# Weighting and adding both expert choices on VectorE after the expert blocks, with GpSimd left to gather

## The chip, the cores and the metric

The kernel runs on one core of one Trainium2 chip. The metric is the device time of one execution in microseconds (us), as the median of several runs. The profile comes from one execution of its own. Lines such as L723 are lines of the kernel before.

## What is computed

Two layers over x (1354 rows of 256 floats), each added to its input:

```python
x = x + attention(layernorm(x), adj, ...)          # softmax(q k^T / 16 + 2 adj) v
x = x + moe(layernorm(x))                          # 8 experts, each row goes to 2

scores = xf @ router_w + router_b
topk_p, topk_i = top_k(softmax(scores), 2)
h = xf @ w1[e] + b1[e]
y = (silu(h @ wg[e] + bg[e]) * (h @ wv[e] + bv[e])) @ w2[e] + b2[e]
out = sum over the two chosen experts of gate * y
```

The change is in the last line: the two gated expert results of each row are added to x.

## The kernel before

The rows are held in 11 tiles of up to 128 rows (`TILES`; the last tile has 74 rows). The attention part ends with each row's two experts known; a row's first choice is the one with the lower expert number, its second choice the one with the higher. Each row is scattered twice into `expert_rows`, sorted by expert, and the rows of an expert fill blocks of 128. `BLOCKS` is 29, the most that any routing can need; where a routing needs fewer, the steps that are left repeat the last block.

The expert part is a loop over the blocks, `experts(s)`, written out on each engine and kept in step by semaphores. TensorE (PE) multiplies block s by the expert's fused gate and up matrices (`bT` against `weights`), transposes the gated result of block s-1 and multiplies block s-2 by the down matrix (`gT` against `weights`, counted by `y_mm`). VectorE (DVE) adds the biases, forms the gated product and the low parts of the split operands, and at L1780 adds the last bias into `ysum` (counted by `y_sum`). ScalarE (ACT) does silu and the high parts, and issues at L982 the store of `ysum` to `expert_out` (`ys`, counted by `y_out`).

GpSimd (POOL) first splits the experts' weights (`product_lo`, `down_lo`). Then it gathers: for choice k = 0 and all tiles, and then for choice k = 1 and all tiles, it reads from `needs` how many blocks must have been stored, waits for `y_out`, and issues at L723 an indirect DMA that brings each row's result into `picked[:, t, k, :]` (semaphore `gathered[t][k]`). Between these gathers it runs `add_first(t)`, three tiles behind the gathers: `picked` times the gate in place (L707), and then that added to `x1` (L710). The semaphore `part_added` counts both steps.

VectorE runs its whole block loop first. Then come eleven calls of `add_second(t)`, one instruction each (L1743): x1 = picked * gate + x1 for the second choice, after `gathered[t][1]` and `part_added`. It counts `added`.

SyncE (SP) writes the result in three stores: tiles 0 to 4 when `added` is 5, tiles 5 to 9 when it is 10 (both L543, 640 KB each), and the last tile with its 74 rows when it is 11 (L546, 74 KB). It then waits for all three:

```python
HALF = TILES // 2
for t in (0, HALF):
    sp.wait_ge(added, t + HALF)
    sp.dma_start(out[...], x1[:, t:t + HALF, :]).then_inc(result_out, 16)
sp.wait_ge(added, TILES)
sp.dma_start(out[span(TILES - 1, LAST), :], x1[:LAST, TILES - 1, :]).then_inc(result_out, 16)
sp.wait_ge(result_out, 48)
```

Of the kernel before, what the change touches and what calls it, by code (L numbers as in the profile page):

```python
# [6 lines left out]
ALU = mybir.AluOpType  # L7
# [40 lines left out]
def attention_then_top2_experts(  # L48
# [4 lines left out]

    N, D = x.shape
    E, _, H = w1.shape
    TOPK = 2
    TILES = -(-N // P)
# [29 lines left out]
    def width(t):  # L87
        return LAST if t == TILES - 1 else P
# [4 lines left out]
    with ExitStack() as ctx:  # L93
        def sem(name):
            return ctx.enter_context(nc.semaphore(name))
# [23 lines left out]
        x1 = keep.place("x1", [P, TILES, D])  # L119
# [41 lines left out]
        gates = keep.place("gates", [P, TOPK, TILES])  # L161
# [100 lines left out]
        picked = moe.place("picked", [P, TILES, TOPK, D])  # L262
# [70 lines left out]
        gathered = [[sem(f"gathered{t}_{k}") for k in range(TOPK)] for t in range(TILES)]  # L333
        part_added, added, result_out = sem("part_added"), sem("added"), sem("result_out")
# [26 lines left out]
        def finish_factors(wait_ge, engine, g, queue):  # L361

            mean, _, var, y, tmp, shift = factors_of(g)
            count = 14 * g

            def step(ins):
                nonlocal count
                count += 1
                ins.then_inc(newton1, 1)
                wait_ge(newton1, count)  # L370
            wait_ge(rough1, 2 * g + 2)
            for _ in range(3):
                step(engine.tensor_tensor(tmp, y, y, ALU.mult))
                step(engine.tensor_tensor(tmp, tmp, var, ALU.mult))
                step(engine.tensor_scalar(tmp, tmp, -0.5, 1.5, ALU.mult, ALU.add))
                step(engine.tensor_tensor(y, tmp, y, ALU.mult))
            step(engine.tensor_tensor(tmp, mean, y, ALU.mult))
            step(engine.tensor_scalar(shift, tmp, -1.0, None, ALU.mult))
            queue.sem_inc(factors_done)
# [171 lines left out]
        def _(pool):  # L551
            G = nc.gpsimd
# [147 lines left out]
                product_lo(e)  # L700
                down_lo(e)

            def add_first(t):

                n = width(t)
                pool.wait_ge(gathered[t][0], 16)
                G.tensor_scalar(picked[:n, t, 0, :], picked[:n, t, 0, :], gates[:n, 0, t:t + 1], None, ALU.mult  # L707
                                ).then_inc(part_added, 1)
                pool.wait_ge(part_added, 2 * t + 1)
                G.tensor_tensor(x1[:n, t, :], x1[:n, t, :], picked[:n, t, 0, :], ALU.add).then_inc(part_added, 1)  # L710


            for k in range(TOPK):
                for t in range(TILES):
                    if k == 0 and t >= 3:
                        add_first(t - 3)
                    if k == 1 and t < 3:
                        add_first(TILES - 3 + t)
                    n = width(t)
                    done = pool.value_load(needs[0:1, k, t:t + 1], min_val=1, max_val=BLOCKS)  # L720
                    pool.wait_ge(y_out, 16 * done)
                    pool.sem_inc(pool_passed)
                    pool.indirect_dma_start(  # L723
                        out=picked[:n, t, k, :], out_offset=None, in_=ys,
                        in_offset=bass.IndirectOffsetOnAxis(ap=ypos_i[:n, t, k:k + 1], axis=0)
                    ).then_inc(gathered[t][k], 16)
# [628 lines left out]
        def _(dve):  # L1355
            V = nc.vector
# [27 lines left out]
            def rough_factors(g):  # L1384
                _, var, half, y, _, _ = factors_of(g)
                V.tensor_scalar(half, var, EPS, None, ALU.add).then_inc(rough1, 1)
                dve.wait_ge(rough1, 2 * g + 1)
                rough_rsqrt(y, half).then_inc(rough1, 1)
# [347 lines left out]
            gate_weights()  # L1736
            dve.sem_inc(tables_done)

            def add_second(t):
                n = width(t)  # L1740
                dve.wait_ge(gathered[t][1], 16)
                dve.wait_ge(part_added, 2 * t + 2)
                V.scalar_tensor_tensor(x1[:n, t, :], picked[:n, t, 1, :], gates[:n, 1, t:t + 1],  # L1743
                                       x1[:n, t, :], ALU.mult, ALU.add).then_inc(added, 1)

            def bias_part(e, p):
                return tile_of(bias[:, :, B_AT[p]:B_AT[p] + B_SIZES[p]], e % B_SLOTS, P)
# [34 lines left out]
            for s in range(BLOCKS + 2):  # L1782
                experts(s)
            for t in range(TILES):
                add_second(t)


# [21 lines left out]
```

## Time and profile before

| | |
|---|---|
| time, median of 3 runs | 422.5 us (420.83 to 422.7) |
| the profiled execution's own time | 422.16 us |
| its span from first to last instruction | 420.4 us |
| TensorE busy | 383.6 us, 91% of the span |
| VectorE busy | 310.5 us, 74% |
| GpSimd busy | 277.3 us, 66% |
| ScalarE busy | 178.5 us, 42% |

The span is what the trace shows; the execution's own time is 1.7 us longer. The median is another 0.3 us above that execution. A busy share is an average over the whole span: it doesn't tell which engine sets the end of the last stretch, and the change lies in that stretch.

### The profile page before, as it was taken

The numbers are of one execution on the slowest core, as the hardware profiler recorded it, in microseconds if no ns is written. First come the engines' busy times: TensorE is split into PE (matmuls) and PEld (weight loads), VectorE is DVE, ScalarE is ACT, GpSimd is POOL, SyncE is SP. The second block draws the span as 40 slices with busy tenths as digits, with TensorE's granted clock in tenths as the row PEclk, the third lists the DMA queues.
The fourth block names the chain that finished last, engine by engine and source line by source line (L and its number), as shares of the span: only waits on it lengthen the run. The fifth ranks groups of instructions, "written<-read, shape, count | busy, mean of one in ns | idle before, by whom it ended". The sixth has DMA issues, their size and how long they took to land.

```text
span 420.4 us, 8132 instructions
## 1 busy us (share of the span) xinstructions
PE 383.6 (91%) x2273; PEld 331.5 (79%) x2273; DVE 310.5 (74%) x737; ACT 178.5 (42%) x312; POOL 277.3 (66%) x303
## 2 busy tenths in 40 slices
PE   1899989999999999999999696799899999999980
PEld 1788869879889889899788475688788888888870
DVE  4686887977779889698896994577576766676754
ACT  1375584463653553554453362453233223333310
POOL 3743949977386596596597650896986740577771
PEclk9899999999999999999999998899999999999996
DMA  6871569878879789688769956547764722233245
GB/s 209 304 276 51 170 222 326 268 202 269 263 222 301 242 245 322 219 258 268 216 215 339 372 171 209 209 140 245 276 248 150 274 87 74 88 92 90 69 128 177
DMA packets 54485, 89.43 MB, mean 213 GB/s; under 512 B 4658, under 2 KB 34810, under 8 KB 53420
## 3 DMA queue, kind: packets, MB, share of 16 engines
q1 hardware_dynamic: 43044, 75.33, 53.6%
q10 hardware_dynamic: 8776, 8.03, 5.9%
q0 software_dynamic: 2624, 5.56, 4.5%
q8 instruction: 21, 0.34, 0.3%
q14 instruction: 20, 0.16, 0.1%
HBM read 56.13 MB, written 32.77 MB: 211 GB/s over the span
## 4 chain that ended last, share of the span: by engine, by line
PE 64%; DVE 12%; DMA 9%; issue 7%; POOL 4%; POOLq 1%; ACT 1%; DVEq 1%; ACTq 0%
PE ps L997 25%; PE ps L1306 19%; PE ps L1201 6%; DMA xblk<-expert_rows 3%; DVE acc L1418 3%; PE ps L1203 3%; PE ps L1149 2%; PE ps L1340 2%; DMA expert_out<-ysum 2%; PE ps L1282 1%; DMA picked<-expert_out,ypos_i 1%; PE ps L1051 1%; DMA expert_rows<-xn_all,posi_all 1%; POOL picked L723 1%; POOLq L720 1%
## 5 line engine op out<-in xcount | busy, mean ns | idle before, releaser
L592 POOL TENSOR_TENSOR lo<-raw,hi 128x512 fp32r<-128x512 f32 x62 | 80.9, 1333 | 53.1 <-DVE acc L1418 48.7
L1306 PE MATMUL ps<-weights,bT_hi 128*128 x232 | 73.2, 397 | 0.0
L997 PE MATMUL ps<-hi,w1T_lo 128*128 128x512 f32 x128 | 53.1, 414 | 1.1 <-DVE w1T_lo L1359 1.0
L1306 PE MATMUL ps<-weights,bT_lo 128*128 x116 | 49.2, 425 | 2.1 <-DVE bT_lo L1359 2.1
L997 PE MATMUL ps<-hi,w1T_hi 128*128 128x512 f32 x128 | 50.7, 396 | 0.0
L1306 PEld LDWEIGHTS ps<-weights,bT_hi 128*128 128x128 f32 x232 | 44.5, 192 | 7.8
L997 PE MATMUL ps<-lo,w1T_hi 128*128 128x512 f32 x128 | 50.4, 394 | 0.0
L1201 PE MATMUL ps<-v,pT_hi 128*128 128x256 f32 (+3 forms) x242 | 44.8, 286 | 0.7 <-DVE pT_lo L1359 0.7
L1754 DVE TENSOR_TENSOR ps<-ps,bias 128x512 f32<-128x512 f32 x29 | 20.3, 699 | 32.6 <-PE ps L1306 25.2
L1418 DVE SCALAR_TENSOR_TENSOR acc<-raw,b1T,acc 128x512 f32<-128x512 f32 x48 | 42.0, 874 | 1.4
L1306 PE MATMUL ps<-weights,gT_hi 128*128 x232 | 42.7, 282 | 0.0
L723 POOL DMA_INDIRECT picked<-expert_out,ypos_i x22 | 22.7, 1031 | 28.2 <-DMA expert_out<-ysum 20.7
L731 ACT ACTIVATE bT_hi<-ps 128x256 fp32r<-128x256 f32 x29 | 11.2, 385 | 70.4 <-PE ps L1282 70.4
L1201 PEld LDWEIGHTS ps<-v,pT_hi 128*128 128x128 f32 (+3 forms) x242 | 36.9, 186 | 0.9 <-DVE pT_lo L1359 0.9
L731 ACT ACTIVATE ring<-ps 128x512 f32<-128x512 f32 x28 | 16.7, 595 | 48.0 <-PE ps L997 46.5
L1306 PE MATMUL ps<-weights,gT_lo 128*128 x116 | 35.2, 304 | 1.5 <-DVE ysum L1780 1.5
L1306 PEld LDWEIGHTS ps<-weights,gT_hi 128*128 128x128 f32 x232 | 36.0, 190 | 0.0
L681 POOL TENSOR_TENSOR weights<-landed,weights 128x2048 fp32r<-128x2048 f32 x7 | 32.2, 4605 | 3.3 <-ACT weights L731 2.9
L1203 PE MATMUL ps<-v,pT_lo 128*128 128x256 f32 (+3 forms) x121 | 34.1, 282 | 0.0
L617 POOL DMA_INDIRECT expert_rows<-xn_all,posi_all x22 | 24.9, 1132 | 8.9 <-issue 4.8
L731 ACT ACTIVATE hi<-raw 128x2048 fp32r<-128x2048 f32 x16 | 30.4, 1899 | 0.0
L1359 DVE TENSOR_TENSOR pT_lo<-ps,pT_hi 128x512 fp32r<-128x512 f32 (+5 forms) x44 | 20.3, 502 | 12.5 <-ACT pT_hi L731 12.5
(226 smaller groups left out, 969.2 us busy)
## 6 DMA issues: line engine op xcount, KB each, us to landing
expert_rows<-zeros SPq DMA_DIRECT2D x11, 1024.0 KB, 10.4
raw<-in_L_ffn_wg SPq DMA_DIRECT2D x8, 1024.0 KB, 6.5
raw<-in_L_ffn_wv SPq DMA_DIRECT2D x8, 1024.0 KB, 7.4
products<-ring SPq DMA_DIRECT2D x28, 256.0 KB, 5.6
landed<-products SPq DMA_DIRECT2D x7, 1024.0 KB, 7.6
adj_sb<-in_adj SPq DMA_DIRECT2D x10, 677.0 KB
bias<-biases SPq DMA_DIRECT2D x8, 640.0 KB, 5.2
w1raw<-in_L_ffn_w SPq DMA_DIRECT2D x8, 512.0 KB, 5.3
```

Source lines behind the costliest of these rows:

```text
L592: G.tensor_tensor(lo[j % RAWS][:, k, :], raw[j % RAWS][:, k, :], r32(hi[j % HIS][:, k, :]), ALU.subtract).then_inc(m_lo, 1)
L617: pool.indirect_dma_start(out=xs, out_offset=bass.IndirectOffsetOnAxis(ap=posi_all[:n, t, k:k + 1], axis=0), in_=xn2_all[:n, t, :], in_off ...
L681: G.tensor_tensor(weights[:, e % SLOTS, AT_LO:AT_LO + C_SIZE], landed[:, e % SLOTS, AT_LO:AT_LO + C_SIZE], r32(weights[:, e % SLOTS, AT_HI ...
L723: pool.indirect_dma_start(out=picked[:n, t, k, :], out_offset=None, in_=ys, in_offset=bass.IndirectOffsetOnAxis(ap=ypos_i[:n, t, k:k + 1], ...
L731: return nc.scalar.activation(o, i, ACT.Copy)
L997: last = nc.tensor.matmul(o, a, b, start=begins and n == 0, stop=ends and n == len(m) - 1)
L1201: nc.tensor.matmul(ps[:n, MIX, 0:D], pT[0][:w, k, :n], v[:w, k, i, :], start=k == 0 and i == 1, stop=False)
L1203: last = nc.tensor.matmul(ps[:n, MIX, 0:D], pT[1][:w, k, :n], v[:w, k, 0, :], start=False, stop=k == TILES - 1)
L1306: last = nc.tensor.matmul(o, stationary[i][:, k, :], part(e, ats[j] + k * width, width), start=n == 0, stop=n == len(m) - 1)
L1359: return V.tensor_tensor(o, a, b, ALU.subtract)
L1418: V.scalar_tensor_tensor(acc[j % ACCS][:, :], buf[:, k, :], b1T[:, e * KH + k:e * KH + k + 1], first_row[:, :] if k == 0 else acc[j % ACCS ...
L1754: V.tensor_tensor(ps[:, BANK_G[s % 2], :], ps[:, BANK_G[s % 2], :], bias_part(e_gu, 0), ALU.add).then_inc(g_sum, 1)
```

## The change

GpSimd keeps the 22 gathers and loses its 22 arithmetic instructions. VectorE's eleven `add_second` become 22 calls of `add_choice`: after the block loop it adds the first choice of all 11 tiles, and then the second choice of all 11. The instruction is the same for both. `part_added` now counts VectorE's first-choice adds, and only the second-choice adds wait for it. `added`, on which the stores wait, still counts the second-choice adds alone.

```diff
-            def add_first(t):
-                n = width(t)
-                pool.wait_ge(gathered[t][0], 16)
-                G.tensor_scalar(picked[:n, t, 0, :], picked[:n, t, 0, :], gates[:n, 0, t:t + 1], None, ALU.mult
-                                ).then_inc(part_added, 1)
-                pool.wait_ge(part_added, 2 * t + 1)
-                G.tensor_tensor(x1[:n, t, :], x1[:n, t, :], picked[:n, t, 0, :], ALU.add).then_inc(part_added, 1)
             for k in range(TOPK):
                 for t in range(TILES):
-                    if k == 0 and t >= 3:
-                        add_first(t - 3)
-                    if k == 1 and t < 3:
-                        add_first(TILES - 3 + t)
                     n = width(t)
                     done = pool.value_load(needs[0:1, k, t:t + 1], min_val=1, max_val=BLOCKS)
                     pool.wait_ge(y_out, 16 * done)
...
-            def add_second(t):
-                n = width(t)
-                dve.wait_ge(gathered[t][1], 16)
-                dve.wait_ge(part_added, 2 * t + 2)
-                V.scalar_tensor_tensor(x1[:n, t, :], picked[:n, t, 1, :], gates[:n, 1, t:t + 1],
-                                       x1[:n, t, :], ALU.mult, ALU.add).then_inc(added, 1)
+            def add_choice(t, k):
+                n = width(t)
+                dve.wait_ge(gathered[t][k], 16)
+                if k == 1:
+                    dve.wait_ge(part_added, t + 1)
+                V.scalar_tensor_tensor(x1[:n, t, :], picked[:n, t, k, :], gates[:n, k, t:t + 1],
+                                       x1[:n, t, :], ALU.mult, ALU.add).then_inc(added if k else part_added, 1)
...
             for s in range(BLOCKS + 2):
                 experts(s)
             for t in range(TILES):
-                add_second(t)
+                add_choice(t, 0)
+            for t in range(TILES):
+                add_choice(t, 1)
```

## Rows read from the trace of the kernel before

**Rows 1.** The page's head: the span, and each engine's busy time.

```profile
span 420.4 us, 8132 instructions
PE 383.6 (91%) x2273; PEld 331.5 (79%) x2273; DVE 310.5 (74%) x737; ACT 178.5 (42%) x312; POOL 277.3 (66%) x303
```

**Rows 2.** The chain that ended last, 398 to 421 us: start, length, what.

```profile
410.78 5.59 DMA picked<-expert_out,ypos_i
416.40 0.48 DVE x L1743
```

**Rows 3.** Timeline of GpSimd, 290 to 421 us: start, length, instruction, [idle before].

```profile
365.65 1.02 POOL L723 DMA_INDIRECT picked<-expert_out,ypos_i  x1 [0.61 <-issue]
366.72 0.93 POOL L707 TENSOR_SCALAR picked<-picked,gates 128x256 f32<-128x256 f32 x1
367.73 0.74 POOL L710 TENSOR_TENSOR x<-x,picked 128x256 f32<-128x256 f32 x1
369.08 1.02 POOL L723 DMA_INDIRECT picked<-expert_out,ypos_i  x1 [0.61 <-issue]
...
402.01 0.96 POOL L723 DMA_INDIRECT picked<-expert_out,ypos_i  x1 [0.31 <-issue]
403.27 0.95 POOL L723 DMA_INDIRECT picked<-expert_out,ypos_i  x1 [0.30 <-issue]
```

**Rows 4.** Timeline of VectorE after its block loop.

```profile
410.16 0.42 DVE L1780 TENSOR_TENSOR ysum<-ps,bias 128x256 f32<-128x256 f32 x1 [2.22 <-DMA expert_out<-ysum]
410.50 4.04 DVE L1743 SCALAR_TENSOR_TENSOR x<-picked,gates,x 128x256 f32<-128x256 f32 x10
416.40 0.48 DVE L1743 SCALAR_TENSOR_TENSOR x<-picked,gates,x 74x256 f32<-74x256 f32 x1 [1.86 <-DMA picked<-expert_out,ypos_i]
```

**Rows 5.** By tile `gates`: the add's duration, ns min/median/max.

```profile
L1743 DVE SCALAR_TENSOR_TENSOR x<-picked,gates,x x11: 474/476/483, 410.5 to 416.4; 128x256 f32<-128x256 f32 x10, 74x256 f32<-74x256 f32 x1
```

**Rows 6.** Windows: each engine's busy time in one stretch, clock, DMA share, GB/s.

```profile
352.00:399.90 47.90, 47.90 (x299) 41.88 (x298) 32.78 (x59) 15.83 (x30) 31.88 (x35) 1.00 0.29 87
```

**Rows 7.** Groups of VectorE by form, 352 to 363 us, then 364 to 399 us.

```profile
L1768 DVE TENSOR_TENSOR gated<-ps,silu 128x512 f32<-128x512 f32 x2 | 1.4, 691 | 0.1
...
L1768 DVE TENSOR_TENSOR gated<-ps,silu 128x512 f32<-128x512 f32 x7 | 4.8, 691 | 0.2
```

**Rows 8.** Timeline: last down multiply and `ysum`, of block 25 and of 29.

```profile
394.75 0.40 PE L1306 MATMUL ps<-weights,gT_hi 128*128 x2
...
395.37 0.42 DVE L1780 TENSOR_TENSOR ysum<-ps,bias 128x256 f32<-128x256 f32 x1
...
409.55 0.40 PE L1306 MATMUL ps<-weights,gT_hi 128*128 x2
```

**Rows 9.** By tile `out`: the result's stores, issue ns, first and last start.

```profile
L543 SPq DMA_DIRECT2D out<-x x2: 388/388/388, 412.6 to 414.6; - x2
L546 SPq DMA_DIRECT2D out<-x x1: 299/299/299, 416.9 to 416.9; - x1
```

**Rows 10.** Windows over the stores: the last two figures are DMA share and GB/s.

```profile
413.40:413.80 0.40, 0.00 (x0) 0.00 (x0) 0.40 (x2) 0.00 (x0) 0.00 (x0) 0.50 0.78 207
...
417.20:417.40 0.20, 0.00 (x0) 0.00 (x0) 0.00 (x0) 0.00 (x0) 0.00 (x0) 0.50 1.02 343
417.40:417.60 0.20, 0.00 (x0) 0.00 (x0) 0.00 (x0) 0.00 (x0) 0.00 (x0) 0.50 0.41 133
...
418.60:419.40 0.80, 0.00 (x0) 0.00 (x0) 0.00 (x0) 0.00 (x0) 0.00 (x0) 0.50 0.23 79
419.40:419.80 0.40, 0.00 (x0) 0.00 (x0) 0.00 (x0) 0.00 (x0) 0.00 (x0) 0.50 0.05 18
```

**Rows 11.** DMA issues: a 74-row gather (388 to 392 us), and all 22.

```profile
picked<-expert_out,ypos_i POOLq DMA_INDIRECT x1, 4.8
...
picked<-expert_out,ypos_i POOLq DMA_INDIRECT x22, 2.9
```

**Rows 12.** Waits of VectorE, 399 to 421 us: in total, times, longest.

```profile
DVE ysum L1780 <- DMA expert_out<-ysum: 3.0, 2, 2.2
```

## The prediction

> **What bounds the kernel now.** The page's head comes first [rows 1]: TensorE is busy 91% of the span, VectorE 74%, GpSimd 66%. That is an average, and the change touches the end alone, so the question is who sets the end. The chain that ended last gives it [rows 2]: its last two pieces are the landing of the last gather (issued 410.78, landed 416.37) and one VectorE add behind it. The reader is to see that this gather is the only add's input that came late. The timeline of GpSimd says why it was issued so late [rows 3]: in the first choice's part a gather comes every 3.43 us (365.65 against the next at 369.08, which the three rows between fill: 1.02 gather, 0.93 multiply, 0.74 add, and the gaps), in the second choice's part every 1.25 us (402.01, 403.27). GpSimd is never caught up from 365 us on.
>
> VectorE is in its block loop until 410.58, then does ten adds at one go, waits 1.86 us for the gather, does the eleventh and ends at 416.88 [rows 4]. The windows say what the block loop is bound by [rows 6]: from 352.0 to 399.9 TensorE is busy 47.90 of 47.90 us at the full granted clock. And the stores say what comes last [rows 9, 10]: two of 640 KB issued at 412.6 and 414.6, one of 74 KB at 416.9, and the span ends at 420.43, 3.5 us after that last issue.
>
> **What the change removes.** 11 multiplies and 11 adds leave GpSimd, 11 x (0.94 + 0.74) = 18.5 us of its time [rows 3]. No block waits for them. The gathers come no later than now, since each has less in front of it. The worst case is the present one: issued 410.78, landed 416.37, and the add that needs it now stands 22nd in VectorE's row, after 418 us (below). So the 1.86 us wait for the gather goes, whatever happens on GpSimd. I expect more: counted from the reference's own inputs, 26 of the 29 blocks are real and the last three steps repeat one, so the last gathers need the store of block 26 only and should be issued before 408 us.
>
> **What it adds.** Eleven more instructions of a form that the trace has, 476 ns each alone [rows 5]. Ten in a row took 4.04 us [rows 4], so one behind another costs (4.04 - 0.476) / 9 = 0.396 us; they overlap. Both kinds of wait in the new row are long satisfied (first choices gathered before 400 us, `part_added` counted eleven instructions earlier), so I take 0.396 and keep 0.476 as the upper bound. Nothing hides these adds: they stand behind the whole block loop on the engine that sets the end. The row starts at 410.50 as now.
> - 5th second-choice add: now ended at 410.50 + 4 x 0.396 + 0.476 = 412.56 (the store was issued at 412.6). It becomes the 16th instruction: 416.92. The first store is late by 11 x 0.396 = 4.36 us.
> - 10th: from 414.54 to 418.90, and the second store as well by 4.36 us.
> - last: 410.50 + 21 x 0.396 + 0.476 = 419.29, against 416.88: 2.41 us late, being 4.36 less the 1.95 us between the tenth add's end and the eleventh's present place in the row (the wait that goes and its start).
>
> **Which of the two counts.** This is where I choose. If only the last add counted, the end would come 2.4 us later; if the first store counts, 4.4. The windows over the stores decide [rows 10]. The first store's data start at about 413.45 (207 GB/s in 413.40 to 413.80), some 0.87 us after its issue, and the big flow ends at about 417.45 (share 1.02 in 417.20 to 417.40, 0.41 in the next window). So two stores of 640 KB need 4.0 us of all 16 DMA engines, 2.0 each, and they are issued 2.0 us apart: they form one unbroken flow. Behind it there is a thin tail at 79 GB/s and a share of 0.23 until about 419.5, some four engines of 16, and the end comes at 420.43, 2.98 us after the flow's end. That tail is the small store, on few engines, with whatever was left. Rows that fit it: a gather of 74 rows took 4.8 us from issue to landing where the median of all 22 is 2.9 [rows 11], so few rows are slow, not quick. The last gather (also 74 rows, 5.59 us) was still under way during the flow, and I read the other part of the tail as the stores' rows that it held up.
>
> The Trainium skill has a rule for this (DMA: Bandwidth & Descriptors, section Why a DMA increments its semaphore by 16 and not by 1): a copy is split over the largest number up to 16 that divides its slowest dimension, so 74 partitions run on 2 engines and 128 on all 16. The thin tail agrees in kind; by the rule the small store must wait on two engines for their share of the big stores, and the end goes with the flow's end.
>
> Now the new order. The first store is issued at 416.94 and its data flow from 417.8; both big stores end at 421.8 (before: 413.45 to 417.45). The small store is issued at 419.33, in the middle of that flow, so it stands behind it on its own engines. Before, it was issued at 416.91 and could have flowed from about 417.78, 0.33 us after the flow had ended; that gap is gone now. End: 421.8 + 2.98 - 0.33 = 424.45, and without taking off the gap 424.8. The difference to 420.43 is 4.0 to 4.4; I take 4.1. The held-up rows of the last gather don't count for this, as they lay beside the small store and not before it.
>
> **The sum.** Adds before the first store +4.36, gap before the small store -0.3: +4.1 us. The profiled execution took 422.16 us and becomes 426.3; the median of the runs is 0.34 above that execution, so the median becomes 426.6, or 1.0% more. A change under 0.5% (2.1 us) can't be told from none here.
>
> **What costs nothing.** GpSimd's freed time (its cover is TensorE's loop, unbroken to 400 us [rows 6]); the denser gathers of the first choice, which need stores of earlier blocks and spread over them. Should they disturb the stores or row loads, TensorE has no slack and each us would be seen; ten gathers 1.25 us apart over the last blocks are in the trace now, and the last `ysum` starts 0.21 us after the last down multiply has ended, as block 25's does 0.22 us after its own [rows 8]. So their density costs nothing there now.
>
> **The rivals.**
> - *The small store is not held by the big ones.* It flows on engines of its own and ends 3.52 us after its issue, as now: 419.33 + 3.52 = 422.85, +2.4, median 424.9. For it: now it also ended 3.5 us after its issue, so the trace alone can't tell. Against it: the big flow had a share of 1.0, leaving no free engine.
> - *VectorE's block loop ends sooner, not slower than before.* The trace puts 2.22 us of waiting before the last `ysum` down to a store of `expert_out` [rows 4], and 3.0 us in the two last waits of this kind together [rows 12]. If the gathers held that store up, gathers that are done earlier would give back up to 3.0 us there: 4.1 - 3.0 = +1.1, median 423.6, within the bound. It decides from 2.0 us given back. Against it: the 0.21 us after the multiply [rows 8], which names TensorE as the releaser. The other way to the same place is that GpSimd's arithmetic slowed VectorE: the product of L1768 takes 691 ns without it (352 to 363 us) and 691 ns with it [rows 7], so nothing is to be had. The Trainium skill (GPSIMD Engine Reference, Specifications) has the two engines contend where VectorE reads two SBUF inputs; this product reads one from PSUM, and the trace agrees that it isn't touched.
> - *The adds don't overlap, or VectorE stalls for its instructions.* At 0.476 us each the 5th second-choice add ends at 410.50 + 16 x 0.476 = 418.1, 5.6 us late: median 428.0. Against it: the ten in a row of now.
>
> **How the numbers follow.** The forecast holds with 0.72 (+3.4 to +4.7 by the uncertainty of the flow's start and end, 426.0 to 427.2); the free small store 0.12; the sooner block loop 0.08; the slower adds 0.05; anything else 0.03. The range takes in the free small store and part of the slower adds: 424.6 to 427.6. Slower by over 0.5%: all of the forecast and the slower adds, and most of the free small store (2.4 against a bound of 2.1): 0.88. Same: the rest of it and the sooner loop: 0.10. Faster: 0.02; it would need the whole row of adds to be paid back, for which no row speaks.
>
> **What would show it.** In the changed profile VectorE's row of adds starts at about 410.5, has 22 members over 8.8 us and no wait for a gather; GpSimd's gathers stand with waits on `expert_out` between them, the last issued before 408 us; TensorE's windows are as before; L543 is issued at 416.9 and 418.9, L546 at 419.3; the flow's share stays at 1.0 for 4.0 us without a break. The end at 424.5 or so says that the first store counts; an end 3.5 us after L546, at 422.9, says that the small store runs free. The prediction is wrong if the block loop's end moves by more than 0.5 us, or the adds' spacing differs from 0.40 us.

## The result and the profile after

The changed kernel is slower: 428.23 us median (426.57 to 432.49, 4 runs) against 422.6 us for the kernel before in the same comparison, a ratio of 1.0145 with a 95% interval of 1.0088 to 1.0202. The forecast was 426.6 us, in a range of 424.6 to 427.6, and slower by more than 0.5% with a chance of 0.88. The direction held; the time lies above the range. One of the four runs, 432.49 us, is 3.7 us above the next; without it the ratio of the means would be 1.0117. A few executions of either kernel are some per cent slower than the rest; they are left out of the ratios, but not of the medians.

The head of the page of the changed kernel, for [rows 1]:

```profile
span 426.8 us, 8121 instructions
PE 385.5 (90%) x2273; PEld 333.4 (78%) x2273; DVE 313.0 (73%) x748; ACT 178.6 (42%) x312; POOL 258.3 (61%) x281
```

The span is 6.4 us longer. GpSimd has lost 19 us of work (the forecast had 18.5), VectorE shows 2.5 us more in sum over the span. TensorE's loop is as it was: busy 47.90 of 47.90 us from 352.0 to 399.9, as before [rows 6].

```profile
352.00:399.90 47.90, 47.90 (x296) 41.75 (x295) 32.93 (x60) 15.50 (x30) 14.84 (x15) 1.00 0.30 91
```

Now VectorE's timeline behind its block loop, for [rows 4]:

```profile
409.26 0.42 DVE L1768 TENSOR_TENSOR ysum<-ps,bias 128x256 f32<-128x256 f32 x1 [0.81 <-DMA expert_out<-ysum]
411.91 0.42 DVE L1768 TENSOR_TENSOR ysum<-ps,bias 128x256 f32<-128x256 f32 x1 [2.23 <-PE ps L1293]
412.26 8.78 DVE L1731 SCALAR_TENSOR_TENSOR x<-picked,gates,x 128x256 f32<-128x256 f32 x22
```

Two things are to be seen. The row of 22 adds lasts 8.78 us without a gap, so its forecast (8.8 us at 0.396 a piece) held to the hundredth. And it starts at 412.26 where the row of before started at 410.50 [rows 4]: 1.76 us were lost before the code that was changed in this stretch came to run. The wait of 2.2 us before the last `ysum` is there as before, but its name is now TensorE and not a store of `expert_out` [rows 4]. So the name it had was not to be trusted, and no time came back from there.

GpSimd, for [rows 3]: the gathers now stand with waits between them, and the last is issued at 409.63, 2.6 us before the row of adds starts. The forecast said before 408; the row itself began 1.76 us later than it assumed, and in the kernel without the first-choice adds (below), where the row starts at 410.54, the last gather is issued at 407.92.

```profile
378.92 0.96 POOL L710 DMA_INDIRECT picked<-expert_out,ypos_i  x1 [2.96 <-DMA expert_out<-ysum]
383.46 0.96 POOL L710 DMA_INDIRECT picked<-expert_out,ypos_i  x1 [3.58 <-DMA expert_out<-ysum]
...
409.63 1.35 POOL L710 DMA_INDIRECT picked<-expert_out,ypos_i  x1 [0.35 <-DMA expert_out<-ysum]
```

The stores, by tile `out`, for [rows 9]:

```profile
L543 SPq DMA_DIRECT2D out<-x x2: 388/388/389, 418.7 to 420.7; - x2
L546 SPq DMA_DIRECT2D out<-x x1: 487/487/487, 421.1 to 421.1; - x1
```

From the row's start to the first store it is 6.43 us (before: 412.58 - 410.50 = 2.08): 4.35 more, forecast 4.36. From the row's start to the end of the span it is 426.8 - 412.26 = 14.5 us against 420.4 - 410.5 = 9.9: 4.6 more, forecast 4.1. The windows over the stores, for [rows 10] (the last two figures are the DMA share and GB/s):

```profile
421.40:423.40 2.00, 0.00 (x0) 0.00 (x0) 0.00 (x0) 0.00 (x0) 0.00 (x0) 0.50 0.97 325
423.40:423.60 0.20, 0.00 (x0) 0.00 (x0) 0.00 (x0) 0.00 (x0) 0.00 (x0) 0.50 0.88 272
423.60:424.00 0.40, 0.00 (x0) 0.00 (x0) 0.00 (x0) 0.00 (x0) 0.00 (x0) 0.50 0.13 18
424.00:425.00 1.00, 0.00 (x0) 0.00 (x0) 0.00 (x0) 0.00 (x0) 0.00 (x0) 0.50 0.11 19
425.00:426.00 1.00, 0.00 (x0) 0.00 (x0) 0.00 (x0) 0.00 (x0) 0.00 (x0) 0.50 0.13 47
```

The flow of both big stores ends at 423.6, 4.9 us after the first store's issue; that distance was the same before (412.58 to 417.45). Behind it only the small store is left, at a share of 0.11 to 0.13, which is two engines of sixteen. Before, the tail had 0.23, as much as four engines. I read them as the small store's two and two that the last gather had made late; for that speaks that the share is 0.11 to 0.13 here, where the gather came early.

So the result falls into two parts: 4.6 us in the end of the program, and in this execution some 1.8 us before it. The experiments take them apart.

### The profile page after: what moved, and what is told of

It reads as the page before. It is cut to its first block, busy times and chain, and to the rows that moved or that the text cites. A ratio compares the mean times of both kernels' runs of the same rounds, so it can differ in the third digit from the quotient of the medians.

```text
span 426.8 us, 8121 instructions
## 1 busy us (share of the span) xinstructions
PE 385.5 (90%) x2273; PEld 333.4 (78%) x2273; DVE 313.0 (73%) x748; ACT 178.6 (42%) x312; POOL 258.3 (61%) x281
## 4 chain that ended last, share of the span: by engine, by line
PE 68%; DVE 12%; DMA 9%; issue 5%; ACT 1%; POOL 1%; ACTq 1%; DVEq 1%; POOLq 0%
PE ps L984 25%; PE ps L1293 23%; PE ps L1188 6%; DMA expert_out<-ysum 4%; DMA xblk<-expert_rows 3%; PE ps L1190 3%; DVE acc L1405 3%; PE ps L1327 2%; PE ps L1136 2%; PE ps L1269 1%; PE ps L1038 1%; DVE x L1731 1%; DMA expert_rows<-xn_all,posi_all 1%; DMA bias_rows<-in_L_gnn_bq 1%; PE ps L1146 1%
```

## The experiments

Each was timed in five rounds against the kernel before. Beside the ratio, one figure is read from each profile: from the start of the row of adds to the end of the span. It leaves out whatever happened before that row.

**The kernel before, against itself.** No edit.

> The kernel before, unchanged, against itself. Theory A (of the change's extra time some 4.5 us belong to the row of adds and the stores behind it, and the 1.8 us by which the changed kernel's row of adds began later come from the first 22 us, which vary from execution to execution): ratio 1.000 with an interval of about 0.5% each way, and in its profile the last bias add of the block loop may start anywhere from 410 to 413 us. Theory B (the first 22 us are slower in the changed kernel as such): the kernel before has the fast start again, within 0.3 us of 410.2 us.

Ratio 0.9999 (0.9964 to 1.0033). Its single executions went from 420.18 to 425.42 us. In its profile, the page's head and VectorE's timeline:

```profile
span 423.7 us, 8132 instructions
```

```profile
413.35 0.42 DVE L1780 TENSOR_TENSOR ysum<-ps,bias 128x256 f32<-128x256 f32 x1 [2.22 <-DMA expert_out<-ysum]
413.69 4.04 DVE L1743 SCALAR_TENSOR_TENSOR x<-picked,gates,x 128x256 f32<-128x256 f32 x10
```

The row of the unchanged kernel starts at 413.69, 3.2 us later than in the first profile and later than in the changed kernel's. Theory A is right that the start moves by itself, but not on the place. At 300 us this execution was still level with the first profile (a `ysum` at 300.28 against 300.40); at the fifth `ysum` after that it was 2.9 us behind (329.38 against 326.47). Between the two TensorE waited for the rows of a block. First the kernel before in its first profile, then this execution: TensorE's wait, and a window of TensorE alone (busy time, clock, DMA share, GB/s).

```profile
302.85 0.44 PE L1282 MATMUL ps<-ident,xblk 128*128 128x128 f32 x2 [1.28 <-DMA xblk<-expert_rows]
304.70:307.90 3.20, 3.20 (x23) 1.00 0.18 63
```

```profile
304.21 0.44 PE L1282 MATMUL ps<-ident,xblk 128*128 128x128 f32 x2 [2.77 <-DMA xblk<-expert_rows]
304.70:307.90 3.20, 3.20 (x11) 0.50 0.02 8
```

The wait is 1.5 us longer, and behind it the granted clock is the lower one (1.2 GHz): 11 matmuls in 3.2 us in place of 23, which I estimate at 3.2 x 12 / 23 = 1.7 us. Three of the 14 profiles have such a wait there, of 2.6 to 2.8 us, with the clock at 0.50 behind it: this one, one of the changed kernel and one of the kernel before with a wide gather. From the row's start to the end it is 10.0 us again.

**The changed kernel twice more.** No edit.

> The changed kernel, unchanged, timed again. Theory A: ratio to before 1.010 to 1.011 (4.5 us), the row of adds lasting 8.8 us and the span ending 14.5 us after its start, wherever that start is. Theory B: ratio 1.014 to 1.016 (6.3 us) again, and the row of adds starting near 412.3 us again.

> The changed kernel once more, unchanged, since its two ratios so far (1.0145 and 1.0195) both lie above the 1.011 that its end explains. If only the end is longer (14.55 against 9.95 us from the start of the row of adds to the end of the span): ratio 1.008 to 1.014, and the row's start again anywhere from 410 to 413.5 us. If the changed kernel loses 2 to 3 us more before the row: 1.016 to 1.020.

Ratios 1.0195 (1.0139 to 1.0251) and 1.0098 (1.0058 to 1.0138). The rows of adds started at 411.64 and 413.25 and the spans ended at 426.2 and 427.8, so both times 14.55 us lay between. The first ratio lies above what either theory had and so nearer to B, with a row that started early, which is against B; the second ratio is against B. The three ratios of the changed kernel, weighted by their intervals, give 1.0134, or 5.7 us, give or take 1.2; the intervals of the last two don't overlap, so the true uncertainty is larger. The 4.6 us of the end (1.0109) lie just inside. What the profiles say on the rest: the last `ysum` started, in the four kernels that keep GpSimd's arithmetic, at 410.16, 413.35, 411.55 and 413.00 (mean 412.0), and in the ten that don't at 411.91, 411.30, 412.90, 410.20, 411.34, 412.96, 411.86, 411.93, 411.34 and 408.06 (mean 411.4). No loss before the row shows in them; the scatter does.

**Eleven adds more in the kernel before, and nothing else.**

```diff
+        extra = sem("extra")
...
+            for t in range(TILES):
+                n = width(t)
+                V.scalar_tensor_tensor(xn2_all[:n, t, :], xn2_all[:n, t, :], gates[:n, 0, t:t + 1],
+                                       xn2_all[:n, t, :], ALU.mult, ALU.add).then_inc(extra, 1)
             for t in range(TILES):
                 add_second(t)
```

> The kernel before with eleven more adds of the same form on VectorE, into a tile that nobody reads any more, ahead of the eleven second-choice adds; GpSimd keeps its arithmetic and its late gathers. It adds the eleven instructions and nothing else. If the row's length alone makes the change's price: the first store is issued 4.36 us later, the row ends at 8.8 us, the wait for the last gather is hidden; ratio as that of the changed kernel, 1.010 to 1.011. If the denser gathers or GpSimd's freed time cost something as well, it stays below the changed kernel by 1 us or more.

Ratio 1.0159 (1.009 to 1.0229), wide, and it holds the changed kernel's. VectorE's timeline is sharper:

```profile
411.89 4.43 DVE L1787 SCALAR_TENSOR_TENSOR xn_all<-xn_all,gates 128x256 f32<-128x256 f32 x11
416.24 4.43 DVE L1744 SCALAR_TENSOR_TENSOR x<-picked,gates,x 128x256 f32<-128x256 f32 x11
```

The row lasts 8.8 us and the span ends at 426.4, 14.5 us after its start: all of the changed kernel's end, with GpSimd's work and its late gathers still in place. The wait for the last gather is gone here too, hidden behind the longer row. So the row's length alone makes the 4.6 us of the end.

**The change without the first-choice adds.** The output lacks the first choice.

```diff
-                if k == 1:
-                    dve.wait_ge(part_added, t + 1)
...
-            for t in range(TILES):
-                add_choice(t, 0)
```

> The changed kernel without the eleven first-choice adds (the first choice's result is left out of the output): GpSimd only gathers, and VectorE does what it did before. It shows what the freed GpSimd brings alone. By my theory only the small store's wait for the last gather goes, and the two big stores' flow, which starts as before, still holds the end: -0.3 to -0.8 us, ratio 0.998 to 0.999. If the last gather was the real end (the chain that ended last says so), the 1.9 us wait comes back whole: ratio 0.9955.

Ratio 1.003 (0.9995 to 1.0065). Its row took 4.43 us with no wait, against 6.38 before [rows 4]: the small store is issued 4.5 us after the row's start in place of 6.4. Yet from the row's start to the end it is 10.2 us, not less than the 9.9 of before. Its stores (by tile `out`) and the windows over them say why:

```profile
L543 SPq DMA_DIRECT2D out<-x x2: 389/389/389, 412.6 to 414.6; - x2
L546 SPq DMA_DIRECT2D out<-x x1: 490/490/490, 415.0 to 415.0; - x1
```

```profile
415.20:417.40 2.20, 0.00 (x0) 0.00 (x0) 0.00 (x0) 0.00 (x0) 0.00 (x0) 0.50 1.00 326
417.40:417.80 0.40, 0.00 (x0) 0.00 (x0) 0.00 (x0) 0.00 (x0) 0.00 (x0) 0.50 0.37 90
417.80:418.80 1.00, 0.00 (x0) 0.00 (x0) 0.00 (x0) 0.00 (x0) 0.00 (x0) 0.50 0.11 14
418.80:419.80 1.00, 0.00 (x0) 0.00 (x0) 0.00 (x0) 0.00 (x0) 0.00 (x0) 0.50 0.13 47
```

The small store is issued at 415.0 and waits for the flow, which ends at 417.5 as before. Then it doesn't start at full pace: 14 GB/s in the first microsecond, 47 in the second. I had expected 0.3 to 0.8 us of gain and found 0.3 us of loss. The chain that ended last named the last gather [rows 2], and to take its wait away brought nothing.

**The small tile first.**

```diff
-            for t in range(TILES):
+            for t in [TILES - 1] + list(range(TILES - 1)):
                 add_choice(t, 1)
...
+            sp.wait_ge(added, 1)
+            sp.dma_start(out[span(TILES - 1, LAST), :], x1[:LAST, TILES - 1, :]).then_inc(result_out, 16)
             for t in (0, HALF):
-                sp.wait_ge(added, t + HALF)
+                sp.wait_ge(added, 1 + t + HALF)
...
-            sp.wait_ge(added, TILES)
-            sp.dma_start(out[span(TILES - 1, LAST), :], x1[:LAST, TILES - 1, :]).then_inc(result_out, 16)
```

> The changed kernel with the 74-row tile's second choice added first and its store issued first, the two big stores behind it. From the start of the row of adds the changed kernel took 14.5 us to the end of the span, with a thin tail of some 2.3 us behind the big stores' flow. If the tail is the small store queued behind the flow on its few engines, it now runs while the flow has not begun, and the end is the flow's own, one add (0.4 us) later than it was: 12.2 to 12.5 us from the start of the row, ratio to before 1.005 to 1.006. If the tail is something else (the big stores' own late rows, the final waits of the queue), it stays: 14.5 to 14.9 us.

Ratio 1.0023 (0.9986 to 1.0059); row start 411.68, span end 424.5, 12.8 us between, 1.7 us less than the changed kernel. It missed the 12.2 to 12.5 by 0.3, but the tail is gone, as its windows over the stores show:

```profile
419.60:423.40 3.80, 0.00 (x0) 0.00 (x0) 1.06 (x3) 0.00 (x0) 0.00 (x0) 0.50 1.00 331
...
423.80:424.50 0.70, 0.00 (x0) 0.00 (x0) 0.00 (x0) 0.00 (x0) 0.00 (x0) 0.50 0.00 0
```

From 423.8 on no byte moves. So the thin tail is the small store, and in another place it costs nothing.

**The last store cut in two.**

```diff
-            sp.dma_start(out[span(TILES - 1, LAST), :], x1[:LAST, TILES - 1, :]).then_inc(result_out, 16)
-            sp.wait_ge(result_out, 48)
+            for a, b in ((0, 64), (64, LAST)):
+                sp.dma_start(out[(TILES - 1) * P + a:(TILES - 1) * P + b, :], x1[a:b, TILES - 1, :]
+                             ).then_inc(result_out, 16)
+            sp.wait_ge(result_out, 64)
```

> The changed kernel with the 74-row store cut in two, 64 rows and 10 rows, in the same place at the end. If 74 rows are slow because they go over two engines, 64 rows over many take 0.2 us of the flow and the end comes 2.0 us sooner: 12.3 to 12.7 us from the start of the row of adds. If the small store's slowness is its place behind the flow and not its width, nothing changes: 14.5 us.

Ratio 1.0076 (1.0045 to 1.0107); row start 413.30, span end 426.1, 12.8 us. The forecast of 12.3 to 12.7 is missed by 0.1. The same rows in the same place cost 1.7 us less when they are cut. So the price needs both: few engines, and the place behind the big stores. To take away either one brings the same 1.7 us. By the Trainium skill's rule (DMA: Bandwidth & Descriptors, Why a DMA increments its semaphore by 16 and not by 1) 74 rows go over 2 engines, 64 over 16 and 10 over 10; the trace agrees, with a share of 0.11 to 0.13 for the 74.

**The adds tile by tile.**

```diff
             for t in range(TILES):
                 add_choice(t, 0)
-            for t in range(TILES):
                 add_choice(t, 1)
```

> The changed kernel with the adds in another order: first and second choice of tile 0, then of tile 1, and so on, still 22 in the row. The second add of a pair waits for the first one's end (0.48 us and a semaphore), so a pair takes about 0.93 us; the first big store is issued at 4.7 us from the row's start in place of 6.4, the second at 9.3 in place of 8.4. If the end goes by the first store's issue, as I had put it, it comes 1.7 us sooner: 12.9 us. If it goes by the last store of the flow, with the flow no longer unbroken: 0.9 us later, 15.4 us, ratio to before 1.013.

Ratio 1.0178 (1.0126 to 1.0231). A pair, the second add of which needs the first, takes 0.98 us (I had expected 0.93), so the row lasts 10.9 us. Its timeline, and its stores by tile `out`:

```profile
408.40 10.90 DVE L1731 SCALAR_TENSOR_TENSOR x<-picked,gates,x 128x256 f32<-128x256 f32 x22
```

```profile
L543 SPq DMA_DIRECT2D out<-x x2: 389/389/389, 413.4 to 418.4; - x2
L546 SPq DMA_DIRECT2D out<-x x1: 299/299/299, 419.3 to 419.3; - x1
```

The first store is issued 5.0 us after the row's start, 1.4 sooner than in the changed kernel; the second 10.0, 1.6 later; and the end comes at 424.5, 16.1 us after the start, 1.5 later. The forecast for this case was 15.4 us, 0.7 too little, and 12.9 if the first store set the end. The end goes with the second big store: from its issue to the span's end it is 6.1 us here, 6.1 in the changed kernel, 6.2 without the first choices and 5.9 in the kernel before.

**The first choices in the block loop,** in VectorE's gaps. The steps are fitted to this input's routing: under another one a gather may need a block that comes later in VectorE's own order, and the kernel would stand still.

```diff
+            first_at = {22: (0, 1), 23: (2, 3), 24: (4, 5), 25: (6, 7), 26: (8, 9), 27: (10,)}
             for s in range(BLOCKS + 2):
                 experts(s)
-            for t in range(TILES):
-                add_choice(t, 0)
+                for t in first_at.get(s, ()):
+                    add_choice(t, 0)
```

> The changed kernel with the eleven first-choice adds put into VectorE's block loop, two behind each of steps 22 to 26 and one behind step 27, in gaps in which VectorE waits 1.07 us for TensorE (a placing that fits this input's routing). If the price is only the row's length at the end, it is that of the kernel without the first choices: 10.3 us from the start of the row to the end, ratio 0.998 to 1.003. If two instructions more in a block disturb TensorE, its block time of 4.87 us grows by 0.1 to 0.8 us for five blocks.

Ratio 0.9995 (0.9955 to 1.0035); row start 412.20, span end 422.4, 10.2 us. The windows from 352.0 to 399.9, for [rows 6]:

```profile
352.00:399.90 47.90, 47.90 (x295) 41.75 (x295) 36.76 (x70) 15.44 (x30) 14.77 (x15) 1.00 0.31 90
```

VectorE has ten instructions more in this stretch than in the changed kernel, and TensorE is busy 47.90 of 47.90 us as before. The pace shows it better than the busy time: from the eighth `ysum` before the last (377.62) to the last (411.86) it is 34.24 us, against 34.26 in the kernel before (375.90 to 410.16). So the eleven adds are free where TensorE sets the pace, and cost 4.4 us where nothing stands beside them.

**Second choices there too, and the last store cut.** The last three steps of the loop repeat a block that is done, so seven second-choice adds were put behind them, two behind step 28 and five behind step 29, on top of the two edits above.

> As the one before, and seven second-choice adds as well in the loop's last steps, which repeat a block that is already done, so that the first big store is issued before the loop ends; the last store cut in 64 and 10 rows. The end: the 74-row gather's landing (1.9 us behind the loop's end), the second big store from 1.3 us and 2.0 us of flow, the last rows behind it: 5.0 to 5.6 us from the loop's end to the span's end against 9.9 in the kernel before, -4.5 us, ratio 0.988 to 0.992. If a store during the last blocks slows them, half of it is lost: ratio 0.994 or more.

Ratio 0.9919 (0.9881 to 0.9957). From the add behind the last `ysum`, at 412.27, to the end at 419.4 it is 7.1 us, 2.8 less than before, but not the 5.0 to 5.6 I expected: VectorE waited 2.23 us for the last gather, which now had the first big store beside it.

**The last tile's gathers over 128 rows,** on top of that one.

```diff
-                    n = width(t)
+                    n = P
                     done = pool.value_load(needs[0:1, k, t:t + 1], min_val=1, max_val=BLOCKS)
```

> As the kernel with both choices in the loop and the last store cut in two, and the last tile's gathers take 128 rows in place of 74 (the rows beyond the 74 are fetched from row 0 and not used). If a gather of 74 rows is slow by its width, the last one now lands 2.8 us after its issue, before the loop ends, and VectorE's 2.2 us wait for it goes: 1.2 to 2.0 us less from the loop's end to the span's end, 5.3 to 5.9 in place of 7.1; ratio 0.987 to 0.990. If it is slow because the first big store flows beside it, the wait stays at 2 us.

Ratio 0.9923 (0.9895 to 0.9951), above the forecast of 0.987 to 0.990: 0.8% faster than the kernel before. The loop's last add started at 411.68 and the span ended at 417.3, 5.6 us, 1.5 less than without the wide gather.

```profile
DMA to landing us min/median/max: 2.7/2.8/2.9
```

This line of the view by tile `picked`, from 400 us on, had a maximum of 5.9 with the 74 rows. The wait is gone from the profile; the ratios of the two kernels don't tell 1.5 us apart.

**The kernel before with a wide last gather and a cut last store,** both free of assumptions on the routing; the two edits are those shown.

> The kernel before, its order of adds kept, with the last tile's gathers over 128 rows and the last store cut in 64 and 10 rows: both are free of any assumption on the routing. The last gather should land 2.9 us after its issue, so that the 1.9 us wait for it shrinks to nothing, and the end should follow the second big store's issue by 4.4 us, as in the changed kernel with the cut store, where it is 5.9 us now: 8.4 to 8.7 us from the start of the row of adds to the end of the span against 9.9, ratio 0.996 to 0.997. If the two engines' rows aren't what holds the end here, 9.9 us and 1.000.

Ratio 0.9971 (0.9934 to 1.0007), a gain of 0.3% that the interval doesn't part from none. The profile is as expected: row start 413.34, span end 421.7, 8.4 us against 9.9.

## Why the prediction was right and wrong

- **What bounds the kernel**: right. TensorE's loop is unbroken to 400 us in both kernels, and nothing that GpSimd gained or lost moved it. The late last gather was rightly seen as no loss that the change could recover in full; even so I still expected 0.3 to 0.8 us from it in the experiment. The kernel without first choices shows its wait to be worth nothing, 10.2 against 9.9 us.
- **The added row**: right. 22 adds in 8.78 us, first store 4.35 us later. Eleven idle adds in the kernel before gave the same end.
- **Which store counts**: the outcome right, the reason wrong as I put it. I wrote that the first store counts. In the changed kernel the two big stores are late by the same 4.36 us, so it couldn't be seen. The tile-by-tile order parts them, and the end followed the second. It is the last full-width store of the flow, with the small one behind it, that sets the end.
- **The gap before the small store**: this term of the sum was wrong, in sign too. I took off 0.3 us because the small store would be waiting when the flow ended. It was waiting, and yet about 0.25 us was lost: from the second big store's issue to the end it is 6.1 to 6.2 us in each kernel where the 74 rows in one store wait behind the flow, and 5.9 in the one before. The gap did go, but a store that waits starts slowly (14 to 19 GB/s in its first microsecond), and the sum had nothing for that; why it starts slowly no run shows. The end measured +4.6, not +4.1.
- **The start of the row**: the sum took it as given ("The row starts at 410.50 as now"), and in the profiled execution it was 412.26. By the prediction's own sign, a block loop's end that moves by more than 0.5 us, it was wrong. The sign was badly chosen: the kernel before moved by 3.2 us against itself. Of the 1.6 us by which the median missed, 0.5 are the gap's term; the rest has no term in the sum, and the runs can't part it from this scatter.
- **The range**: this is what put the result outside. It was made of the bounds of those terms, +2.1 to +5.1 us on one median of 422.5. It held nothing for the rest of the program, where the same code starts its last stretch anywhere between 408 and 413.4 us, nor for how few runs a median has. The medians of the kernel before went from 422.1 to 423.5, those of the changed kernel from 427.56 to 429.75. By ratio the forecast of 1.0% lies inside the first interval (0.9 to 2.0%) and inside that of the third (0.6 to 1.4%), but not of the second (1.4 to 2.5%).
- **The rivals**: the free small store is refuted, as its own issue was followed by the end after 5.7 us (421.1 to 426.8) and not 3.5. The sooner block loop is refuted: the wait before the last `ysum` stayed in every kernel with this loop end, at 2.2 to 2.4 us. The adds that don't overlap are refuted by 8.78 us.

What stays open: the three ratios together lie at 5.7 us, 1.1 above the end's 4.6. Over all ten comparisons of kernels without GpSimd's arithmetic, the ratio lies on average 0.13% above what their end alone would give (row's start to end, less 9.9, in 422.6), 0.6 us give or take 1.1; the kernel before with eleven adds more, which keeps that arithmetic, lies 0.5% above it. So a loss before the row, if there is one, is small. One trace of it can't be ruled out: a slow first 22 us (below) stands in five of the ten profiles without the arithmetic and in none of the four with it, too few to tell a rule from chance.

## What to carry to other kernels

Work taken from an engine with time to spare and put behind the loop of another was paid in full here, though each add took only 0.4 us; the same adds inside the loop that TensorE bounds were free. At the end of a program look at the stores and not at the last wait: here a wait of 1.9 us in the chain that ended last was worth nothing, since two stores of 640 KB stood between it and the end. And where a range is made from one profile, add to the terms' bounds what two executions of the same program differ by.

## What the runs showed of the hardware that was not expected

- A copy of 74 rows was slow by its width. The last gather of 74 rows took 4.5 to 5.9 us to land, and over 128 rows at most 3.1; the store's tail took 1.7 us more than the same rows cut in 64 and 10.
- The first 25 us vary with the moment at which TensorE gets its higher clock. The windows of TensorE alone (busy time, clock, DMA share, GB/s), first of the kernel before, then of the changed kernel:

```profile
17.00:20.00 3.00, 3.00 (x15) 0.50 1.00 353
20.30:22.70 2.40, 2.40 (x24) 1.00 0.60 240
```

```profile
17.00:20.00 3.00, 3.00 (x15) 1.00 0.93 324
20.30:22.70 2.40, 2.40 (x12) 1.00 0.73 292
22.90:24.90 2.00, 2.00 (x19) 1.00 0.00 1
```

  In the kernel before the recorded clock is 0.50 (1.2 GHz) from 17 to 20 us, and when it is 1.00 again the matmuls come twice as fast, 24 in 2.4 us. In the changed kernel they keep the slow pace, 12 in 2.4 us, until 22.8 us, in the same part of the code, though the view says 1.00 there. So the clock of a view should be held against the matmuls' pace. From 16 to 22 us the 14 profiles did 28 or 29 matmuls (five), 37 to 39 (eight) or 50 (one, the tile-by-tile kernel, whose row of adds started soonest, at 408.40).
- The name of a releaser can be wrong: the same 2.22 us before the last `ysum` are put down to a store in the kernel before and to TensorE in the changed one.
